# Second attention's key products moved ahead inside the first 128 recurrence steps, with the rounding of the ternary weights moved behind the first attention's keys

## What is computed

```python
# layer 0, first block: a linear recurrence over 1024 positions, clipped at each
def step(carry, u):
    sr = sr * decay + r * 0.1;  si = si * decay + i * 0.1
    nr = clip(sr * c - si * s, -10, 10);  ni = clip(sr * s + si * c, -10, 10)
x = layernorm(x + recurrence_and_ffn(x))
# layer 0, cross attention ("first attention"): 16 heads, context of 154 positions
x = layernorm(x + xattn(x, ctx, ctx, Wq, Wk, Wv, Wo))
# layer 0, ffn with ternary weights
scale = 1.0 / clip(mean(abs(w)), 1e-05)
wq = clip(round(w * scale), -1, 1) / scale
# layer 1: causal attention, then cross attention ("second attention")
k = einsum('bka,ahc->bkhc', ctx, k_weights)
v = einsum('bka,ahc->bkhc', ctx, v_weights)
# then a quantised gated ffn
```

## Time and profile before

| what | value |
|---|---|
| median of 3 executions | 1998.86 us (1998.55 to 1998.88) |
| the profiled execution's own time | 1991.99 us |
| its span in the trace | 1990.2 us |
| mean granted clock of PE | 0.932 of full speed |
| PE, DVE, ACT, POOL busy | 87%, 69%, 51%, 23% |

### The profile page before, as it was taken

One profiled execution on the slowest core, in us unless ns is written; L12 is line 12 of the kernel. 1 busy time (PEld: TensorE's weight loads), 2 busy tenths in 40 slices (PEclk: granted clock), 3 DMA queues, 4 the chain that ended last, 5 costly groups with the idle time before them and its releaser, 6 DMA issues.

```text
span 1990.2 us, 34704 instructions
## 1 busy us (share of the span) xinstructions
PE 1727.6 (87%) x12889; PEld 1256.4 (63%) x12889; DVE 1380.0 (69%) x4830; ACT 1019.0 (51%) x2647; POOL 463.2 (23%) x501
## 2 busy tenths in 40 slices
PE   3688888888869888999999999999779999979808
PEld 1456666667653455766767766766669989864307
DVE  6877888888335885777776577777566666753785
ACT  5555655555438543555554355555244555533752
POOL 4000000000000223333333234334323333220003
PEclk7798888998979979999999999999889999999859
DMA  5100000000000201000000000000324243300001
GB/s 163 43 1 1 1 1 1 1 1 2 1 1 0 43 21 70 1 1 1 1 2 1 1 1 2 1 1 2 98 64 96 66 96 78 83 1 0 0 0 43
DMA packets 86078, 49.56 MB, mean 25 GB/s; under 512 B 40223, under 2 KB 83669, under 8 KB 85717
## 3 DMA queue, kind: packets, MB, share of 16 engines
q1 hardware_dynamic: 80195, 47.18, 9.1%
q10 hardware_dynamic: 5714, 0.16, 0.2%
HBM read 45.24 MB, written 2.10 MB: 24 GB/s over the span
## 4 chain that ended last, share of the span: by engine, by line
PE 58%; DVE 26%; ACT 9%; issue 4%; POOL 3%; DMA 0%; POOLq 0%; ACTq 0%; DVEq 0%
PE PS L2079 6%; PE PS L1747 6%; DVE nx L774 5%; DVE sq L783 5%; PE PS L1759 5%; PE PS L1772 4%; PE PS L2513 3%; ACT px L1817 3%; PE PS L1733 3%; PE PS L2143 3%; PE PS L1709 3%; PE PS L1787 2%; PE PS L1720 2%; PE PS L2099 2%; PE PS L828 2%
## 5 line engine op out<-in xcount | busy, mean ns | idle before, releaser
L1817 ACT ACTIVATE px<-PS,cnm 128x896 f32<-128x896 f32 (+7 forms) x256 | 189.2, 756 | 285.6 <-DVE cnm L1882 285.6
L1924 POOL TENSOR_SCALAR px<-px,crl 128x640 f32<-128x640 f32 (+7 forms) x128 | 232.3, 1824 | 371.5 <-DVE crl L1893 371.5
L783 DVE TENSOR_SCALAR sq<-nx 128x4 f32<-128x4 f32 x1024 | 175.5, 171 | 31.4
L774 DVE TENSOR_TENSOR_SCAN nx<-sq 128x6 f32<-128x6 f32 x1024 | 174.0, 170 | 32.0 <-POOL sq L913 0.9
L1880 DVE TENSOR_REDUCE cm<-PS 128x1 f32<-128x512 f32 (+3 forms) x224 | 153.9, 687 | 44.6 <-PE PS L1747 44.6
L1759 PE MATMUL PS<-ident,px 128*128 128x128 f32 x1152 | 156.3, 281 | 9.3 <-ACT pT L1830 6.4
L2183 ACT ACTIVATE YT<-YT,xnm 128x154 f32<-128x154 f32 x256 | 104.8, 413 | 92.8 <-DVE xnm L2214 92.8
L198 POOL TENSOR_SCALAR rstd<-mv 128x1 f32<-128x1 f32 x80 | 34.0, 425 | 506.6 <-DVE mv L176 506.5
L1747 PE MATMUL PS<-kT,qT 64*128 64x512 f32 (+3 forms) x768 | 147.9, 503 | 0.4
L1759 PEld LDWEIGHTS PS<-ident,px 128*128 128x128 f32 x1152 | 124.3, 141 | 36.6 <-ACT pT L1830 23.9
L1772 PEld LDWEIGHTS PS<-pT,V 128*64 128x64 f32 x2304 | 124.7, 137 | 34.4 <-issue 32.5
(11 more groups left out here) (336 smaller groups left out, 3855.0 us busy)
## 6 DMA issues: line engine op xcount, KB each, us to landing
xbs<-in_fside_Bx16xSxS SPq DMA_DIRECT2D x8, 1232.0 KB, 6.6
fsrc<-in_fside_Bx16xSxS SPq DMA_DIRECT2D x8, 1232.0 KB, 6.7
xmk<-in_mask_Bx16xSxS_bk SPq DMA_DIRECT2D x8, 308.0 KB, 8.3
fsrc<-in_mask_Bx16xSxS_bk SPq DMA_DIRECT2D x8, 308.0 KB, 8.3
X<-in_x SPq DMA_DIRECT2D x4, 512.0 KB, 6.8
w<-in_L_attn_W_ffn SPq DMA_DIRECT2D x2, 1024.0 KB, 13.0
t<-in_L_ffn_w SPq DMA_DIRECT2D x2, 1024.0 KB, 11.0
out<-xs SPq DMA_DIRECT2D x16, 128.0 KB, 1.7
```

The costliest lines, as they stand in the source:

```text
L774: e.tensor_tensor_scan(k.nx[:, t % 2, :], d0, d1, 0.0, ALU.mult, ALU.add).then_inc(sem("rec.scan"), 1)
L783: e.tensor_scalar(place(c % 2 * 2 * W6 + 6 * n + 7), state, 10.0, -10.0, ALU.min, ALU.max).then_inc(sem("rec.clip"), 1)
L1817: e.activation(k.px[n % 2][:, h, c0:c1], row[:, c0:c1], ACT.Exp, scale=-1.0, bias=k.cnm[:, h, slot:slot + 1], accum_out=k.cl[:, h, slot:sl ...
L1924: e.tensor_scalar(x, x, k.crl[:, 0, slot:slot + 1], None, ALU.mult).then_inc(sem("c.normal0"), 1)
```

## The change

It changes the list of steps and the waits that the new places need.

- The eight `x.key` stand behind steps 101 to 108 of the recurrence, one after each, ahead of `tern_scale`. Before, they stood behind steps 113, 115, up to 127.
- `tern_round` stands behind the eight flips and the four `n.key`, not ahead of them.
- The four `x.value` stand behind steps 112, 116, 120 and 124, ahead of the end of the chunk. Before, they were in the second chunk. Of the two `x.tail`, the first now comes ahead of `tern_int`, the second right behind it.
- The flips of the first attention's weights wait until all eight `x.key` are copied out (they share bank 6). `x.key` waits for the context's flips alone, not for all eight `x0` flips.

```diff
@@ flips_tensor
         if kind in ("x0", "x0q", "x0k"):
             w.wait_ge("load.x0", 16 * 14)
             w.wait_ge("zero", 2)
             w.wait_ge("tails", 1)
+            w.wait_ge("x.kept", HP)
@@ recurrence_order
+    k.contextflipped = sum(by == "scalar" for *_, by in k.flips)
...
-    o.add(*steps(85, 108))
+    o.add(*steps(85, 100))
+    for m in range(HP):
+        o.add(*steps(100 + m, 101 + m), ("x.key", m))
     o.add(("tern_scale",))
     o.add(*steps(108, 109))
     o.add(("tern_inverse",))
-    o.add(("tern_round",))
     x0 = [n for n in third if k.flips[n][0] in ("x0", "x0q", "x0k")]
     o.add(*[("flip", n) for n in x0])
     o.add(*[("n.key", m) for m in range(4)])
-    o.add(*steps(109, 111))
-    for m in range(HP):
-        o.add(*steps(111 + 2 * m, 113 + 2 * m), ("x.key", m))
-    o.add(*steps(111 + 2 * HP, C))
+    o.add(("tern_round",))
+    first = 109
+    for n in range(4):
+        o.add(*steps(first, 112 + 4 * n), k.ahead[HP + n])
+        first = 112 + 4 * n
+    o.add(*steps(first, C))
@@ first_chunk
-    yield 1, ahead[HP]
+    yield 1, ahead[-2]
     yield 3, ("tern_int",)
-    for n, step in enumerate(ahead[HP + 1:]):
-        yield 4 if n else 1, step
-    yield GAPS["value"] - 1 - 4 * (len(ahead) - HP - 1), ("n.value", 0)
+    yield 1, ahead[-1]
+    yield GAPS["value"] - 5, ("n.value", 0)
@@ cross_tensor
-        w.wait_ge("flip.scalar", k.x0flipped)
+        w.wait_ge("flip.scalar", k.x0flipped if n >= HP else k.contextflipped)
```

## The result

| what | before | with the change |
|---|---|---|
| median of 6 executions each, taken in turn | 1998.87 us | 2005.17 us (2000.67 to 2006.6) |
| ratio | | 1.0028 (1.0015 to 1.0041) |
| the profiled execution's own time, its span | 1991.99, 1990.2 us | 2004.62, 2002.8 us |
| mean granted clock | 0.932 | 0.925 |

The change is slower by 0.28%, just over what can be told. By the prediction's own sign, a move of over 4.0 us, it was wrong in the first and the third (5.6 and 5.0 us by the ratios) and right in the second (1.0 us).

What follows compares the result with a forecast made beforehand. It took the bound to be when PE reaches the norm and how fast it then goes to the scores. An earlier norm (-1.8) and a clock fall (+2.5) gave +0.7 on 1998.86: 1999.6 us, no change, range 1993.0 to 2004.5.

Steps and rivals of the forecast that it cites:

- Keys, flips, first attention's keys: First chunk on PE: keys from 72.72 end at 83.1, eight flips at 88.0, first attention's keys at 92.15.
- Rounding, values, states: ACT rounds from 92.85 to 96.9, PE waits 1.9 us for a bank, states copied 101.7 to 103.4, 2.3 later.
- without a pause: Reading of the kernel before: ACT, late by 14.8 us, works through tern_int to the norm at 111.64 without waiting.
- DVE's waits: The 4.68 us wait for the first attention's values goes; the 3.90 at the first scores becomes 9.3.
- Norm's transposes: PE's transposes for the norm ahead of up come at 114.3 against 116.13, 1.8 us earlier.
- Clock at the gap: PE idles 3.1 us ahead of the norm's transposes; the clock falls, costing 2.1 on up and 0.4 on transposes: +2.5.
- Rival 1: The clock holds at the new gap, so the chain keeps its 1.8 us: 1997.1 us; chance 0.17.
- The rule that the prediction quoted: Clock falls only at idle gaps over a certain length; 3.1 us is under it, so the clock holds, sum -1.8.
- The sum: At the first scores: -1.8 from the earlier norm plus 2.5 from the clock's fall gives +0.7 us.
- Rival 3: A second fall, at the flips or PE's wait at 95.6, 2.1 us each; with both 2003.8 us, slower; chance 0.22.
- Behind it all engines go on as before, 0.7 later: After the first scores nothing else moves, so the profiled 1991.99 us simply becomes 0.7 us more.
- Rival 2: Five later chunks' waits, 4.5 us together, go if the clock holds there: say 1993.9 us, faster; chance 0.24.

Runs made afterwards that it cites:

- the first and the third: Two of three comparisons of the unchanged changed kernel against the kernel before: ratios 1.0028 (2005.17 us) and 1.0025 (2000.45 us).
- the second: The changed kernel once more, unchanged, against the kernel before: 1998.6 us, ratio 1.0005 (0.9996 to 1.0014).
- keys only: The eight x.key moved early, rounding and values where they were, against the kernel before: 1991.77 us, ratio 0.997 (0.9956 to 0.9985).
- values back: The changed kernel with values and tails put back, keys early and rounding behind n.key, against the kernel before: 1995.46 us, ratio 0.9991.
- rounding only: The kernel before with only the rounding moved, behind the flips and n.key, against the kernel before: 1996.73 us, ratio 0.9987 (0.9971 to 1.0003).
- new order: Keys early, rounding between flips and n.key, two values ahead of the states and two behind, against before: 0.9981; with dummy products 0.9983.
- the first comparison: The changed kernel against the kernel before, six executions each: 2005.17 against 1998.87 us, ratio 1.0028 (1.0015 to 1.0041).
- the one with the dummy: Keys alone moved, with one dummy product behind the norm's transposes, against the kernel before: 1995.95 us, ratio 0.999 (0.9977 to 1.0002).
- the second group: Runs on one chip beside the kernel before: change again 1.0005, values back 0.9991, before with one dummy product 0.9986, new order 0.9981.
- the two filled ones: The changed kernel with four dummy products in PE's gaps, run twice against the kernel before: 1998.53 us, 1.0001, and 1998.31 us, 1.001.

## Why the prediction was right or wrong

**Keys, flips, first attention's keys.** Predicted 83.1, 88.0 and 92.15; measured 83.58, 87.6 and 92.49. A flip takes 0.91 a pair of four rows, where I took 0.96. The clock came back at 77.40, 4.6 us into the keys, near the 4.24 taken from the earlier trace rows.

**Rounding, values, states.** Predicted: states copied from 101.7 to 103.4, PE's wait of 1.9 in the middle of the values. Measured: 101.76 to 103.46, and 1.61. The start of the norm on ACT came at 110.29 for 110.05. One reading under it was wrong: in the kernel before, ACT did not work "without a pause" up to the norm, but waited twice for PE's values and tails:

```profile
108.59 0.59 ACT L2164 COPY xV<-PS 128x512 f32<-128x512 f32 x1 [1.34 <-PE PS L2066]
110.45 1.16 ACT L2170 COPY xVr<-PS 26x512 f32<-26x512 f32 x2 [1.28 <-PE PS L2073]
```

So the late states held that norm by way of PE (`from`, values, tails), and not by ACT's list. It did not hurt the forecast, which added up ACT's list for the new order, where the values stand ahead of the states.

**DVE's waits.** Right: the 4.68 went, to 0.21, and came back at the first scores: 10.18 for 9.3.

**Norm's transposes.** The first mis-sized term: -1.8 us predicted, -1.13 measured. Of the 0.70 between 114.3 and 115.00, 0.24 came with ACT's later start, and 0.46 are one operation on POOL, told in the last section.

**Clock at the gap.** Right in kind and nearly in size. I had 3.1 us of idle and +2.5 (0.4 and 2.1); it was 3.58 of idle and 0.38 + 1.92 = 2.30. Rival 1 falls: the clock did not hold in any of three traces of the change. Nor did it at gaps of 3.54 (keys only) and 4.42 (values back). It held at the lone gaps of 1.61 (the change, among the values) and 2.80 (rounding only). The rule that the prediction quoted from the Trainium skill (TensorE: Matmul & The Clock Gate, HAM oscillation) was applied to a gap of 3.1 us that did not occur. The gap was 3.58, and the three gaps at which the clock fell, 3.54, 3.58 and 4.42, are all past the length that the page names, so there the traces agree with it. What the rule does not cover are the falls behind shorter gaps: 1.45 and 1.69 us with the transposes between (new order), and 1.69 alone in two traces of five. Of the 0.48 us by which the gap outgrew the forecast, 0.46 are the POOL operation; whether the clock would have held at 3.1 no run shows. The page's other statement, that the place of the change differs from run to run, agrees with the 5.42 and 7.11 us of two traces of one kernel.

**The sum.** Here the prediction missed. "Sum at the scores: -1.8 + 2.5 = +0.7" came out as +2.2 on PE. The missing 1.5 us: 0.7 from the transposes above and 1.3 from the fall at 128.60 (3.25 for 1.95) that I had not priced, less 0.2 by which the first fall was smaller and 0.3 behind it, where the clock came back at 152.49 and not at 155.74. On DVE's row of the scores, by which the prediction told its wait, the same return of the clock left +1.38. Rival 3 had the mechanism, a second fall, and a size of 2.1 for each. It named the flips and PE's wait at 95.6, where the window shows 1.00 throughout. So a second fall came, at another place and on the path. That the upper end of the range, 2004.5, lies so near the median is luck: rival 3 set it with falls at places where none came, and of the 6.3 us between the medians of the first comparison the traces show 2.2 at the first scores.

**"Behind it all engines go on as before, 0.7 later".** Wrong as a method. From the first scores to the ternary ffn, traces of *one* kernel took 442.0 and 446.0 us (before), or 445.2, 449.3 and 449.4 (changed). Each has falls at its own places: in the kernel before the clock is 1.00 from 503 to 518 us and 0.51 from 548 to 569; in the kernel after it is 0.54 from 503 to 518. So of the 12.6 us between the two shown spans, 2.2 lie ahead of the first scores, 7.4 between there and the ffn, and 3 behind it, the last two in stages that the change does not touch.

**Rival 2** falls: the later waits stayed, at 1.03 to 1.34 us.

**What stays open.** How much slower the change is. Against the better trace of before it costs 2.2 us at the scores, against the other one it gains 0.5; three comparisons gave +0.28%, +0.05% and +0.25%, and 2.2 us are 0.11%. Filling the gap took 3.7 and 3.3 us off at the scores; against the third run of the change on the same chip the median fell by 2.1 us only, and the intervals overlap. Whether the change makes falls likelier in later chunks (449.4, 445.2, 449.3 against 442.0 to 449.4 in the others) can't be settled with one trace of each run. The granted clocks of all executions do not settle it either: their mean was 0.9300 with the change and 0.9293 before in the second group, and 0.9275 and 0.9287 in the third.

**Which part did harm.** Keys early bring the scores 1.3 and 1.4 us sooner than the better trace of before; for the time, one comparison shows a gain (0.997) and the one with the dummy does not (0.999, up to 1.0002). Rounding later brings the transposes 4.0 us sooner, and no change of the time that can be told. The values ahead of the states open the gap: put back, on the chip where the change had 1.0005, they gave 0.9991, again with overlapping intervals.

## What to carry to other kernels

Work that looks like filler beside a critical chain may be what keeps PE's clock up. Before moving it away, look at what PE does in the gaps it leaves, and price those gaps as slow products behind them, on the path. A wait on an engine that is only a customer further down is worth nothing if the chain it waits for next is not sooner. And where one kernel's executions spread by 0.6%, take a second trace of the kernel *before* predicting from one: the spread tells what the first trace can't.

## What was not expected of the hardware

**One POOL operation held until a DVE operation ends.** The norm's 128x1 power on POOL takes 0.55 us, save once. The kernel after, all engines:

```profile
112.21 0.55 POOL L207 TENSOR_TENSOR rstd<-rstd,neghalf 128x1 f32<-128x1 f32 x1
...
113.12 1.01 POOL L207 TENSOR_TENSOR rstd<-rstd,neghalf 128x1 f32<-128x1 f32 x1
...
113.41 0.69 DVE L765 TENSOR_SCALAR t1i<-t1i 128x2048 bf16<-128x2048 bf16 x1
...
114.17 0.29 ACT L270 ACTIVATE lst<-lst,rstd 128x1 f32<-128x1 f32 x1 [1.07 <-POOL rstd L207]
```

It is 0.46 us longer where DVE clips the ternary weights in bf16 beside it, and ends with that clip (114.13 and 114.10). The other two runs of the change have 1.01 as well, and the two filled ones 1.09 and 0.95, each ending with its clip too. In the kernel before the clip is at 118.2, and both operations take 0.55; so too with the keys alone and in the new order. ACT waits for it, so it is on the path. The Trainium skill (SBUF — State Buffer, SBUF: two separate sides) says that some DVE operations and any of GpSimd's take one shared port in turn for a whole instruction, and that the first to start keeps it. The rows agree in that one is held until the other ends. They do not agree in the order: POOL's operation began 0.29 us ahead of the clip (113.12 and 113.41) and was the one held, as far as POOL's rows are exact. That this port is the cause was not tested by itself.

**The spread of one kernel.** Twelve executions of the unchanged kernel on one chip lay between 1992.15 and 2003.69 us, with the same instructions in the same order; the two traces differ in where the granted clock fell.
